# A new order of products and a GpSimd low part in an attention kernel on one Trainium2 core

## The reference

```python
q_c = hidden_size @ Wq_c.T + bq_c
q = (q_c @ Wq_up.T + bq_up).reshape(b, s, NH, Q_HEAD).transpose(0, 2, 1, 3)
kv = hidden_size @ Wkv_c.T + bkv_c
...
scores = jnp.einsum('bhqd,bhkd->bhqk', q, k) / np.sqrt(Q_HEAD)
attn = jax.nn.softmax(scores, axis=-1)
o = jnp.einsum('bhqk,bhkv->bhqv', attn, v)
out = jnp.einsum('bhsv,Hv->bsH', o, Wo) + bo
```

## Time and profile before

| | us |
|---|---|
| median of 3 runs | 1736.18 |
| lowest and highest | 1735.65, 1743.07 |
| the profiled execution | 1741.29 |
| its span, first to last instruction | 1739.5 |
| busy in it: PE, DVE, ACT, POOL | 1600.7, 1551.6, 1389.5, 827.2 |

### The profile page before, as it was taken

How to read it: one execution, slowest core, us unless ns; L and a number is a source line. 1 busy time by engine, 2 the same in 40 slices (tenths; PEclk the granted TensorE clock), 3 DMA queues, 4 the chain that set the end, 5 groups by cost and what they waited for, 6 DMA issues and landing times. The chain is left out here.

```text
span 1739.5 us, 23723 instructions
## 1 busy us (share of the span) xinstructions
PE 1600.7 (92%) x7572; PEld 766.7 (44%) x7572; DVE 1551.6 (89%) x2088; ACT 1389.5 (80%) x1979; POOL 827.2 (48%) x1226
## 2 busy tenths in 40 slices
PE   7989999989999999999999999999999999998899
PEld 6734444444444444444444444444444444443354
DVE  6679999989989999999999999999999999999665
ACT  4678888878888888888888888888888888888422
POOL 3334545554545555555545455555545445454320
PEclk9999999999999999999999999999999999999999
DMA  6589999999999999999999999999999999999611
GB/s 224 180 180 199 198 200 207 196 199 189 210 194 190 202 203 197 205 204 200 198 194 197 205 207 186 205 201 205 200 191 193 203 203 198 198 205 193 153 49 49
DMA packets 1092405, 330.86 MB, mean 190 GB/s; under 512 B 1070336, under 2 KB 1076768, under 8 KB 1092288
## 3 DMA queue, kind: packets, MB, share of 16 engines
q1 hardware_dynamic: 1080128, 296.22, 92.6%
q0 software_dynamic: 12160, 33.18, 8.4%
HBM read 50.39 MB, written 10.49 MB: 35 GB/s over the span
## 5 line engine op out<-in xcount | busy, mean ns | idle before, releaser
L925 ACT ACTIVATE S<-S,shift,unscale 128x1024 f32<-128x1024 f32 x512 | 603.4, 1178 | 179.8 <-DVE shift L980 179.0
L973 DVE TENSOR_REDUCE mx<-S 128x1 f32<-128x1024 f32 x512 | 623.0, 1217 | 48.0 <-PE S L825 48.0
L965 DVE TENSOR_TENSOR halves<-S,halves 128x1024 f16<-128x1024 f32 x512 | 624.4, 1220 | 35.9 <-ACT halves L934 28.4
L934 ACT ACTIVATE halves<-S 128x1024 f16<-128x1024 f32 x512 | 523.9, 1023 | 27.6 <-DMA PT<-halves 11.8
L823 PE MATMUL S<-kvTH,qeH 128*128 128x512 f16 x1024 | 391.6, 382 | 46.1 <-DVE halves L965 45.9
L824 PE MATMUL S<-kvTL,qeH 128*128 128x512 f16 x1024 | 388.9, 380 | 0.0
L825 PE MATMUL S<-kvTH,qeL 128*128 128x512 f16 x1024 | 388.8, 380 | 0.0
L763 POOL CAST onormH<-onorm 128x512 fp32r<-128x512 f32 x127 | 77.4, 609 | 510.6 <-DVE onorm L1020 510.6
L836 PE MATMUL O<-PT,kvn 128*128 128x512 f16 x1024 | 243.7, 381 | 59.2 <-issue 42.3
L823 PEld LDWEIGHTS S<-kvTH,qeH 128*128 128x128 f16 x1024 | 99.7, 97 | 231.7 <-DVE halves L965 100.7
L836 PEld LDWEIGHTS O<-PT,kvn 128*128 128x128 f16 x1024 | 91.8, 97 | 210.0 <-issue 118.1
(11 more groups left out here) (261 smaller groups left out, 1878.8 us busy)
## 6 DMA issues: line engine op xcount, KB each, us to landing
weff<-weff_scratch POOLq DMA_DIRECT2D x126, 192.0 KB, 4.6
wv<-in_wv POOLq DMA_DIRECT2D x128, 64.0 KB, 4.0
PT<-halves SPq DMA_TRANSPOSE x512, 5.1
raw<-in_raw SPq DMA_DIRECT2D x8, 772.0 KB, 6.7
weff_scratch<-w_split SPq DMA_DIRECT2D x8, 768.0 KB, 5.0
x<-in_x SPq DMA_DIRECT2D x4, 1024.0 KB, 7.4
x_all<-in_x SPq DMA_DIRECT2D x3, 1024.0 KB, 5.3
out<-y SPq DMA_DIRECT2D x3, 1024.0 KB, 4.3
```

The costliest lines, as they stand in the source:

```text
L925: nc.scalar.activation(S[:, t % SLOTS, :], S[:, t % SLOTS, :], ACT.Exp, bias=shift[:, col:col + 1], scale=keep["unscale"][:, 0:1], accum_o ...
L934: nc.scalar.activation(halves[u][:, 0, :], S[:, t % SLOTS, :], ACT.Copy).then_inc(high_out, 1)
L965: v.tensor_tensor(halves[u][:, 1, :], S[:, t % SLOTS, :], halves[u][:, 0, :], ALU.subtract).then_inc(low_out, 1)
L973: v.reduce_max(mx[:, col:col + 1], S[:, t % SLOTS, :], AX.X, negate=True).then_inc(max_ready, 1)
```

## The change

The first tile of each step (`u == 0`) gets its probabilities in an SBUF tensor `prob0` instead of in its slot of `S`, and the low part of this tile is made by POOL from there, behind the split of `onorm` and ahead of the weight loads. SP and ACT wait for it by a semaphore of its own, `low0_out`; `low_out` counts the other three tiles (`lows(t)`). The slot of the first tile is free as soon as its exp is done.

The order becomes:

- PE: scores 0, row of g - 2, scores 1, values of g - 2, scores 2, scores 3, query projection, output.
- ACT: exp and high part of 0, 1 and 2, copy of q, exp of 3, copy of the row, high part of 3.
- DVE: maximum 0, shift 0, maximum 1, low part of tile 3 of the step before, shift 1, reciprocals, `normalized()`, maximum 2, shift 2, low 1, maximum 3, shift 3, low 2.
- POOL: split of `onorm`, low part of tile 0, loads of `wv` and `weff`, split of `wv`, split of q.

```diff
+        prob0 = sb("prob0", [P, SEQ])
         wvs = sb("wv_scaled", [KVL, VH])
...
         names = ("bv_in", "ones_set", "scores_ready", "max_ready", "shift_ready", "probs_ready",
-                 "high_out", "low_out", "recip_ready", "row_filled", "pv_done", "onorm_ready", "wv_done", "vsum_out",
+                 "high_out", "low_out", "low0_out", "recip_ready", "row_filled", "pv_done", "onorm_ready", "wv_done", "vsum_out",
                  "wv_split", "onorm_high", "onorm_low", "ffn_in", "row_ready", "bo_added", "projected0", "summed0",
                  "stats0", "std0_done", "rstd0_done", "sign_ready", "q_filled", "q_high", "q_copied", "q_low", "row_out")
-        (bv_in, ones_set, scores_ready, max_ready, shift_ready, probs_ready, high_out, low_out,
+        (bv_in, ones_set, scores_ready, max_ready, shift_ready, probs_ready, high_out, low_out, low0_out,
          recip_ready, row_filled, pv_done, onorm_ready, wv_done, vsum_out,
...
+        def lows(t):
+            return (UN - 1) * (t // UN) + t % UN
...
-                sp.wait_ge(low_out, UN * g + u + 1)
+                if u:
+                    sp.wait_ge(low_out, lows(UN * g + u))
+                else:
+                    sp.wait_ge(low0_out, g + 1)
                 sp.dma_start(PT[par][:, :, u * P:(u + 1) * P], halves[u][:].rearrange("p t s -> p (t s)"),
...
             def body(g, b, h, par):
-                if exists(g):
-                    if g >= 2:
-                        pool.wait_ge(wv_split, g - 1)
-                    pool.dma_start(wv[par][:], dram["wv"][h]).then_inc(wv_in[par], 16)
-                if exists(g + 3):
-                    load_weights(g + 3)
                 if exists(g - 2) and exists(g - 1):
...
                     nc.gpsimd.tensor_tensor(onormL[:], onorm[0:KVL, :], f32(onormH[0:KVL, :]), ALU.subtract).then_inc(onorm_low, 1)
+                if exists(g):
+                    pool.wait_ge(high_out, UN * g + 1)
+                    nc.gpsimd.tensor_tensor(halves[0][:, 1, :], prob0[:], halves[0][:, 0, :], ALU.subtract).then_inc(low0_out, 1)
+                    if g >= 2:
+                        pool.wait_ge(wv_split, g - 1)
+                    pool.dma_start(wv[par][:], dram["wv"][h]).then_inc(wv_in[par], 16)
+                if exists(g + 3):
+                    load_weights(g + 3)
                 if exists(g - 1):
...
                         pe.wait_ge(q_low, g + 1)
-                    if t >= SLOTS:
-                        pe.wait_ge(low_out, t - SLOTS + 1)
+                    if t >= SLOTS and (t - SLOTS) % UN:
+                        pe.wait_ge(low_out, lows(t - SLOTS))
+                    elif t >= SLOTS:
+                        pe.wait_ge(probs_ready, t - SLOTS + 1)
                     q = slice(u * P, (u + 1) * P)
...
-                    if g >= 3:
+                    pe.wait_ge(row_out, g - 1)
+                    if not on:
                         pe.wait_ge(onorm_ready, g - 2)
-                    pe.wait_ge(row_out, g - 1)
                     for u in range(UN):
...
                     scores(0)
+                if exists(g - 2) and exists(g - 1):
+                    if exists(g + 1):
+                        pe.wait_ge(q_copied, g + 2)
+                    elif exists(g - 3):
+                        pe.wait_ge(onorm_ready, g - 2)
+                    repeat_row(g - 2, O[:])
+                if on:
+                    scores(1)
                 if g == NG:
-                    pe.wait_ge(low_out, UN * NG - 1)
+                    pe.wait_ge(low_out, lows(UN * NG - 2))
                     project_tile(UN - 1)
...
                 if on:
-                    scores(1)
                     scores(2)
+                    scores(3)
+                    if h == 2 and b:
+                        pe.wait_ge(vsum_out, b)
+                        pe.wait_ge(ffn_in, 16 * 9)
+                        project_tile(b - 1)
                     if exists(g + 2):
...
                         project_queries(g + 2)
-                    if h == 2 and b:
-                        pe.wait_ge(vsum_out, b)
-                        pe.wait_ge(ffn_in, 16 * 9)
-                        project_tile(b - 1)
-                    scores(3)
                     if h == 2:
...
                     output()
-                if on and exists(g - 1):
-                    if exists(g + 2):
-                        pe.wait_ge(q_copied, g + 3)
-                    elif g >= 2:
-                        pe.wait_ge(onorm_ready, g - 1)
-                    repeat_row(g - 1, O[:])
...
             def body(g, b, h, par):
+                def probabilities(u):
+                    return prob0[:] if u == 0 else S[:, (UN * g + u) % SLOTS, :]
...
                     act.wait_ge(shift_ready, t + 1)
-                    nc.scalar.activation(S[:, t % SLOTS, :], S[:, t % SLOTS, :], ACT.Exp, bias=shift[:, col:col + 1],
+                    if g and u == 0:
+                        act.wait_ge(low0_out, g)
+                    nc.scalar.activation(probabilities(u), S[:, t % SLOTS, :], ACT.Exp, bias=shift[:, col:col + 1],
                                          scale=keep["unscale"][:, 0:1],
...
                         act.wait_ge(turned[u], 16 * g)
-                    nc.scalar.activation(halves[u][:, 0, :], S[:, t % SLOTS, :], ACT.Copy).then_inc(high_out, 1)
+                    nc.scalar.activation(halves[u][:, 0, :], probabilities(u), ACT.Copy).then_inc(high_out, 1)
...
                     for u in range(UN):
-                        if u == 2 and exists(g + 2):
+                        if u == 3 and exists(g + 2):
                             copy_q(g + 2)
+                        exp(u)
                         if u == 3 and exists(g - 1):
                             copy_row(O[:])
-                        exp(u)
                         high(u)
...
                         maximum(u)
+                        if u == 1 and one:
+                            low(UN * g - 1)
                         shifted(u)
-                        if UN * g + u:
+                        if u == 1 and one:
+                            reciprocals()
+                        if u == 1 and g >= 2:
+                            normalized()
+                        if u >= 2:
                             low(UN * g + u - 1)
-                        if u == 0 and one:
-                            reciprocals()
-                        if u == 0 and g >= 2:
-                            normalized()
                         if (u, h) == (1, 2) and b:
...
                             v.tensor_copy(keep["vsum"][:, (b - 1) * BLK:b * BLK], V[:]).then_inc(vsum_out, 1)
-                        if (u, h) == (2, 2) and b:
+                        if (u, h) == (3, 2) and b:
                             add_projection(b - 1)
```

## The result

| | before | after |
|---|---|---|
| median, us | 1737.36 | 1778.07 |
| ratio, 95% interval | | 1.0187 (1.0155 to 1.022) |
| profiled execution, its span, us | 1741.29, 1739.5 | 1770.88, 1769.1 |
| granted clock, mean | 0.993 | 0.981 |

Without the one left out, the changed kernel's median is 1775.6 us; that is 1.022 of 1737.4, and 1.0187 of the 1743 us that the kernel before took in the later comparisons. The forecast was 1714 us with 1664 to 1757.

A forecast was written before the change was run, and what follows sets the result against it. The prediction took an 11.73 us chain through several engines as the bound, then the DMA queue: 11.4 plus 0.15 gives 11.55, saving 0.18 us in some 125 heads, 22 us, hence 1714 us from 1736.2; range 1664 to 1757.

The forecast's parts named there:

- DVE's share: On DVE, one low part of four leaves, 1.21 us a head; outside the bounding chain, so alone it buys nothing.
- POOL's low part: On POOL, tile 0's subtraction over 1024 columns, taken at 2.2 us between estimates of 2.09 and 2.54.
- Exp into SBUF: On ACT, tile 0's exp writes SBUF and its high part reads it; taken at nothing, 0.2 us a head at most.
- The old chain: Shift, ACT's exps and row copy, PE's values and scores, DVE's maximum and shift set 11.73 us; the new order breaks it.
- engines at 10.95: In the new order the engines alone, without the DMA queue, would hold a head of 10.95 us.
- the walk: Step-by-step times of PE, ACT, DVE and POOL through one head in the new order, closing at 10.95 us.
- The queue's need: DMA time for a head's four transposes plus weight loads: 11.4 us, bounds 10.7 and 11.7.
- The elastic rival: DMA queue needs only 10.7 us a head, so PE's 10.95 rules; 1639 to 1682 us, chance 17%.
- 0.15 for times when the burst leaves the queue unfed: In the DMA queue, 0.15 us a head added for gaps after bunched transposes, giving a period of 11.55.
- the return of tile 0: ACT's high 0 waits for its transpose, delaying the round; 1757 us, or 1788 with landing 8.2; 20% with slower forms.
- The turn of a block, three times, keeps its own waits: At three block changes in attention, waits stay as before; the 0.18 us gain counts only in some 125 heads.
- No lock: DVE shifts and POOL's low part would not exclude each other; the opposite, up to 275 us added, had 1%.

The follow-up runs named there:

- no_weff: Changed kernel without the loads of weff in attention, each head using the weights of head 0 or 1; 1681.7 us, one run.
- order_only: Changed kernel's new order of all engines, but the first tile's probabilities stay in PSUM and DVE makes its low part; 0.9988 of the kernel before.
- loads_first: Changed kernel with the loads of wv and weff put back to the start of POOL's step; 0.9998 of the kernel before.
- combined: Changed kernel with loads at the start of POOL's step, two buffers for all tiles' halves, and the projected block added at tile 2; 0.9887 of the kernel before.
- two_all: Changed kernel with two buffers for the halves of all four tiles; 1.0009 of the kernel before.
- turn_only: Changed kernel with DVE's addition of the projected block back at tile 2 instead of tile 3; 1.0085 of the kernel before.
- low_first: Changed kernel with POOL's low part of tile 0 ahead of the split of onorm; 0.9994 of the kernel before.

## Why the prediction was wrong

- **DVE's share is worth nothing by itself:** right (low_only 1.0011, which moves the low part to POOL and leaves the order).
- **POOL's low part:** 2.2 us taken, 2.137 measured. **Exp into SBUF:** taken at nothing, 1223 ns against 1172 and 1057 against 1027 for its high part, 0.08 us a head.
- **The old chain broken, engines at 10.95:** right as far as it goes: 31 of 106 steady heads take 10.91 to 10.96 us, and in such a head the walk holds within 0.3 us at each step but high 0.
- **The queue's need:** 11.4 taken, 11.54 measured in the changed kernel. Right within its bounds. The elastic rival (10.7) falls, and no_weff shows that the loads' bytes are in the need: without weff's 192 KB a head it is 10.63.
- **"0.15 for times when the burst leaves the queue unfed":** this is the step that failed, with the return of tile 0 behind it. It was 11.99 - 11.54 = 0.45 us (before 11.80 - 11.60 = 0.20; order_only 0.20, loads_first 0.33, combined 0.23); with the need it makes a period of 11.99 where 11.55 was forecast. I named the three things that set it (late first tile, burst in order, loads right behind) and priced them as a rival with "it exceeds 11.73 from a mean landing of 7.4 us". That is where the reasoning broke: the round was priced at the mean landing. The mean is 6.7, by which the rival gives (16.1 + 6.7)/2 = 11.4, no loss. But a head is hardly ever shorter than 10.91, so early landings give nothing back and a late one (up to 10.8) is paid. The number was in the forecast: tile 0 had 5.1 us to return, and the median landing of all transposes was 5.1. In the trace, the 46 of tile 0's landings that took 7 us or more bring 115 of the 156 us that high 0 waits, 2.5 us each, and the other 81 bring 0.5 each. two_all, in which no high part waits for a transpose any more, has 0.21 in place of 0.45. My own sign for the rival, high 0 waiting over 1 us in most heads, fell just short: 53 of 128. So the way that I gave 20% is what happened, at a mean landing (6.7 us) by which I would have called it harmless.

```profile
DMA to landing us min/median/max: 4.3/5.0/10.8
```

- **"The turn of a block, three times, keeps its own waits":** wrong by 2.8 us each. The change moves DVE's addition behind one more tile, and I didn't follow that edit. turn_only puts the whole step at 1.0187 - 1.0085 = 1.0% (each uncertain by 0.3), and its turns are 14 us shorter than the changed kernel's.
- **The clock:** not foreseen (below).
- **The base of the sum:** the 11.73 is the undisturbed head; the mean of steady heads before is 11.80, so a period of 11.55 would have been worth 0.25 us a head, not 0.18. Small here, but it mixes a least with a mean.
- Added up against the forecast of 1719 for the profiled execution: 22 us of gain that didn't come, 0.19 x 115 = 22 of loss in steady heads, and 8.4 at the turns make 1771; it took 1770.9. This is the split of the traces read back, no second proof.
- **No lock:** right. With POOL 269 us longer at work, no shift on DVE is longer than before:

```profile
L999 DVE TENSOR_SCALAR shift<-mx,unscale,c_lift x512: 261/272/277, 101.6 to 1645.3; 128x1 f32<-128x1 f32 x171
```

What stays open: why a load from POOL's queue slows the transposes for 5 us in some heads and hardly in others (87 GB/s on average with the DMA engines under way), why heads without weff stay at 11.22, and how much of the 30 us is the clock's.

## What to carry to other kernels

Where a resource is nearly full, price a tighter return not by its mean latency but head by head against the floor: the early ones give nothing back. When a producer moves to a later engine, look at everything that is issued in order behind it; here two transposes and two loads moved with one low part. And an order change of many lines is worth taking apart: one line of it (the turn of a block) was about half of the loss, the loads' place alone undid all of it, and with the loads' place and the buffers mended too the same idea gains 1.1%.

## What the runs showed of the hardware

After the stall above, PE's products are longer: 0.58 to 0.63 us instead of 0.38. The granted clock and busy times in four stretches (us, busy of PE, PEld, DVE, ACT, POOL, clock, DMA share, GB/s):

```profile
1165.00:1175.00 10.00, 8.33 (x41) 3.71 (x41) 8.04 (x11) 8.64 (x14) 6.28 (x9) 1.00 1.07 205
1193.00:1196.00 3.00, 1.93 (x5) 0.72 (x6) 2.96 (x4) 2.97 (x5) 2.36 (x6) 0.50 1.03 176
1196.00:1199.00 3.00, 3.00 (x10) 1.60 (x9) 1.99 (x3) 2.09 (x4) 1.40 (x2) 0.50 1.04 243
1202.00:1213.00 11.00, 11.00 (x56) 5.18 (x54) 9.96 (x14) 9.08 (x13) 8.06 (x10) 1.00 0.87 173
```

PE had stood idle from 1191.50, its first product starts at 1194.07; the clock stood at 0.50, 1.2 GHz, from 1193.0 to 1199.8, and at full 2.4 GHz before and after. In the trace's clock records it stands at the lower level for 44 us of the changed kernel's attention and 10 of the kernel before, 20 of combined. By an estimate from these, 34 us more at half speed cost PE up to 17, and it is busy 19.5 longer. The Trainium skill ("TensorE: Matmul & The Clock Gate", "Part 1: The HAM clock gate (the "warmup" mystery)") has 1.2 GHz as the idle engine's level, which activity raises to 2.4; the trace agrees, 0.50 behind the wait and 1.00 from 1202. So a stall that ends in PE can be paid twice. How much of these 17 us reached the end isn't shown: no run holds the clock apart from the stalls. Against much of it stands low_first: its clock is at the lower level for 90 us of attention and PE busy 1620.4 us, as long as in the changed kernel, yet its time is that of the kernel before.
